# Cross-attention in turns of two rounds, its order and buffers rewritten, on one Trainium2 core

## What is computed

```python
x = layer_norm(x, g_norm);  q = x @ Wq                 # 16 heads of 64
k, v = split(context @ Wkv)                            # 128 keys per batch
k = concat([null_kv[0], k]);  v = concat([null_kv[1], v])
sim = where(mask, (q * s) @ (k * s).T, -max)           # 128 x 129 per head
out = softmax(sim) @ v;  out = out @ Wout
return layer_norm(out, g_out)
...
x = x + tanh(g_xattn[1]) * above;  x = x + tanh(g_ffn[1]) * ffn(layer_norm(x))
```

## Time and profile before

| what | value |
|---|---|
| device time, median of 3 runs | 318.1 us (316.18 to 318.48) |
| device time of the profiled execution | 316.18 us |
| its span, first to last instruction | 314.3 us |
| PE busy | 288.2 us (92%) |
| DVE busy | 242.5 us (77%) |
| ACT busy | 231.4 us (74%) |
| POOL busy | 161.3 us (51%) |

### The profile page before, as it was taken

One profiled execution on the slowest core, in us unless ns is written; L12 is line 12 of the kernel. 1 busy time (PEld: TensorE's weight loads), 2 busy tenths in 40 slices (PEclk: granted clock), 3 DMA queues, 4 the chain that ended last, 5 costly groups with the idle time before them and its releaser, 6 DMA issues.

```text
span 314.3 us, 7704 instructions
## 1 busy us (share of the span) xinstructions
PE 288.2 (92%) x2594; PEld 235.7 (75%) x2594; DVE 242.5 (77%) x726; ACT 231.4 (74%) x780; POOL 161.3 (51%) x230
## 2 busy tenths in 40 slices
PE   7688999999999869999999999999999998977765
PEld 6567768686776658889899898898998877742455
DVE  3798999999977427677787787877877878658875
ACT  2777596969899677787787877878878767429290
POOL 2124617243543115556969789686766855553200
PEclk9999999999999999999999999999999999999999
DMA  5841010002020000000000000000000000000004
GB/s 155 198 118 27 1 27 1 0 3 67 3 67 1 2 0 0 2 3 3 2 1 2 2 1 3 2 2 4 1 2 2 1 2 1 2 2 0 1 2 133
DMA packets 11478, 6.67 MB, mean 21 GB/s; under 512 B 3824, under 2 KB 10992, under 8 KB 11440
## 3 DMA queue, kind: packets, MB, share of 16 engines
q1 hardware_dynamic: 10560, 5.99, 6.9%
q10 hardware_dynamic: 880, 0.20, 0.3%
HBM read 5.14 MB, written 1.05 MB: 20 GB/s over the span
## 4 chain that ended last, share of the span: by engine, by line
PE 72%; DVE 11%; ACT 8%; issue 3%; DMA 2%; SPq 2%; POOL 1%; ACTq 0%; DVEq 0%
PE psum L1064 16%; PE psum L1191 10%; PE psum L1497 10%; PE psum L1511 9%; PE psum L1068 7%; PE psum L1070 6%; PE psum L1069 6%; DMA KT<-in_L_ffn_w_down 2%; ACT work L1055 2%; DVE hgm L2150 2%; DVE nmx L1977 2%; SPq L387 2%; PE psum L1598 1%; DVE work L1971 1%; PE psum L1288 1%
## 5 line engine op out<-in xcount | busy, mean ns | idle before, releaser
L990 ACT ACTIVATE work<-psum,nmx 128x129 f32<-128x129 f32 x256 | 83.4, 420 | 22.8 <-DVE nmx L1977 22.8
L574 POOL TENSOR_TENSOR work<-work,rden 128x512 f32<-128x512 f32 x63 | 65.7, 1042 | 46.8 <-DVE rden L1990 46.2
L1064 PE MATMUL psum<-ident,work 128*128 128x128 f32 (+2 forms) x376 | 58.8, 282 | 3.7 <-DVE work L1971 2.6
L1977 DVE TENSOR_REDUCE nmx<-psum 128x4 f32<-128x516 f32 x64 | 41.6, 689 | 25.6 <-PE psum L1191 25.4
L990 ACT ACTIVATION_READ_ACCUMULATOR work<-psum,nmx 128x1 f32 x256 | 58.9, 230 | 0.0
L1068 PE MATMUL psum<-split 97*128 97x512 f32 (+1 forms) x128 | 52.0, 406 | 1.5 <-issue 0.8
L1064 PEld LDWEIGHTS psum<-ident,work 128*128 128x128 f32 (+2 forms) x376 | 41.1, 142 | 13.5 <-issue 3.6
L1971 DVE COPY work<-psum 128x512 f32<-128x512 f32 x63 | 43.2, 686 | 4.1 <-PE psum L1064 0.3
L1070 PE MATMUL psum<-split 97*128 97x512 f32 (+1 forms) x128 | 43.3, 338 | 0.0
L1069 PE MATMUL psum<-split 97*128 97x512 f32 (+1 forms) x128 | 43.2, 338 | 0.0
L1191 PE MATMUL psum<-KT,work 64*128 64x129 f32 x512 | 37.5, 285 | 2.5 <-DVE den L1986 1.8
(11 more groups left out here) (196 smaller groups left out, 532.2 us busy)
## 6 DMA issues: line engine op xcount, KB each, us to landing
KT<-in_L_xattn_Wkv SPq DMA_DIRECT2D x2, 384.0 KB, 4.5
X<-in_x SPq DMA_DIRECT2D x1, 768.0 KB, 5.6
out_x<-X SPq DMA_DIRECT2D x3, 256.0 KB, 2.6
work<-in_ctx SPq DMA_DIRECT2D x3, 192.0 KB, 2.4
work<-in_L_xattn_Wq SPq DMA_DIRECT2D x1, 512.0 KB, 3.6
work<-in_L_xattn_Wout SPq DMA_DIRECT2D x1, 512.0 KB, 4.1
X<-in_x SPq DMA_DIRECT2D x1, 256.0 KB, 3.3
KT<-in_L_ffn_w_gate SPq DMA_DIRECT2D x1, 256.0 KB, 5.7
```

What stands on the lines that cost most here:

```text
L574: pool.tensor_tensor(sx_[:, :, 0:S], sx_[:, :, 0:S], bcast(rden[n % 2][:, :], S), ALU.mult).then_inc(p_ready.sem, 1)
L990: ins = act.activation(Sx[n % 4][:, j, :], psum[:, here, (j // 2) * K1:(j // 2 + 1) * K1], ACT.Exp, bias=nmx[n % 2][:, j:j + 1], accum_out ...
L1064: return pe.transpose(dst, src, ident[0:m, 0:m])
L1977: dve.tensor_reduce(nmx[n % 2][:, :].rearrange("p (c a) -> p c a", a=2), sim, AX_X, ALU.max, negate=True).then_inc(max_done.sem, 1)
```

## The change

The loops go over turns M of two rounds (NT = 16) in place of rounds.
- PE does in turn M: query piece of round 2M, transposes of round 2M-4, output projection of round 2M-6, transposes of round 2M-3, query piece 2M+1, output projection 2M-5, then scores of rounds 2M and 2M+1, then values of rounds 2M-4 and 2M-3. The queries are now of the round whose scores follow in the same turn.
- Transposes go to banks 4 and 5 in turn; the values of a round overwrite its bank (4 or 5) after both were copied. PTs has four buffers, oT two, Sx five.
- The null column is gone: scores have 128 columns; DVE takes the maximum of a whole round in one reduction (128 x 1024), then a small min with 0; ACT computes the null key's exponents with one ACTIVATE of 128 x 8 a round. The row sums go to SBUF (`key_sum`) in place of PSUM. A scores round waits for the exponents of its banks, in place of the denominators.
- ACT does in turn M: exponents of step 4(M-1), the two output copies of rounds 2M-6 and 2M-5, exponents of the second step, query copy, third step, query copy, fourth step, and in every second turn the copy of y.
- DVE and POOL follow the list of rounds with later places; both rounds' pair work stands on DVE behind the third denominators and ahead of the maxima.
- The last pair but one, too, is now finished on DVE after the loop, as is the last.

The diff, cut to its core (removed loops and functions stand in the printed kernel; the splitting of the key and value weights into two buffers each, whose room the new buffers reuse, is left out):

```diff
-        Sx = [work.carve(HPU * K1, n * HPU * K1).rearrange("p (h k) -> p h k", h=HPU) for n in range(4)]
-        PTs = [work.carve(HPU * S) for _ in range(2)]
-        oT = work.carve(4 * S)
+        Sx = [work.carve(HPU * S, n * HPU * S) for n in range(4)] + [late.carve(HPU * S, 0)]
+        Sx = [a.rearrange("p (h k) -> p h k", h=HPU) for a in Sx]
+        PTs = [work.carve(HPU * S) for _ in range(2)] + [late.carve(HPU * S) for _ in range(2)]
+        oT = [work.carve(4 * S), late.carve(4 * S)]
...
         hd = sb("hd", [P, G])
-        nmx = [sb(f"nmx{n}", [P, HPU]) for n in range(2)]
+
+        rmx = [sb(f"rmx{n}", [P, 2 * HPU]) for n in range(2)]
+        nmx = [sb(f"nmx{n}", [P, 2 * HPU]) for n in range(2)]
+        null_exp = [sb(f"null_exp{n}", [P, 2 * HPU]) for n in range(2)]
...
         NR = NS // 2
-        T_LAG, WO_LAG = 2, 3
-        Y_AT = 6
-        Y_STATS_AT, Y_AGGR_AT, RSTD_Y_AT, X3_AT = 6, 7, 7, 8
-        X_STATS_AT, X_AGGR_AT, RSTD_X_AT, XN4_AT, GM_AT = 9, 10, 10, 11, 12
+        NT = NR // 2
+        Y_AT, Y_STATS_AT, Y_AGGR_AT, RSTD_Y_AT, X3_AT = 9, 10, 11, 11, 12
+        X_STATS_AT, X_AGGR_AT, RSTD_X_AT, XN4_AT, GM_AT = 13, 14, 14, 15, 17
...
+            def pair_work(m):
                 if 9 <= m < 21 and m % 2 == 1:
                     down_weights((m - 9) // 2)
                 t = pair_at(m, RSTD_Y_AT)
                 if t is not None:
                     rstd_y(t)
+                    y_affine(t)
                 t = pair_at(m, X3_AT)
                 if t is not None:
                     y_gain(t)
                     residual(t)
                 t = pair_at(m, RSTD_X_AT)
                 if t is not None:
                     rstd_x(t)
-                t = pair_at(m, 1)
+                t = pair_at(m, SPLIT_AT)
+            for M in range(NT + 1):
+                for k in range(2):
+                    for n in range(4 * (M - 1) + 2 * k, 4 * (M - 1) + 2 * k + 2):
+                        if 0 <= n < NS - 1:
+                            normalise(n)
+                    pair_work(2 * M + k)
+            rstd_x(NPAIR - 3)
+            rstd_y(NPAIR - 2)
             rstd_x(NPAIR - 2)
             rstd_y(NPAIR - 1)
             rstd_x(NPAIR - 1)
...
+            def o_evac(r):
+                act.wait_ge(ot_done.sem, ot_done.at(2 * r + 2))
+                if r >= 2:
+                    act.wait_ge(wo_done.sem, wo_done.at(2 * r - 2))
+                act.activation(oT[r % 2], bank[4 + r % 2], ACT.Identity, bias=nv_col[:, 0:1]).then_inc(ot_out.sem, 1)
...
+                r, h = divmod(n, 2)
+                act.wait_ge(max_done.sem, max_done.at(r + 1))
+                if h == 0:
+                    act.activation(null_exp[r % 2][:, :], nmx[r % 2][:, :], ACT.Exp)
+                if n >= 5:
+                    act.wait_ge(pt_done.sem, pt_done.at(n - 4))
                 for j in range(HPU):
+                    at, col = 2 * h + j // 2, column(h, j)
+                    ins = act.activation(Sx[n % 5][:, j, :], bank[2 * (r % 2) + j % 2][:, at * S:(at + 1) * S], ACT.Exp,
+                                         bias=nmx[r % 2][:, col:col + 1], accum_out=key_sum[r % 2][:, col:col + 1])
                 ins.then_inc(exp_done.sem, 1)
+            for M in range(NT + 1):
+                n = 4 * (M - 1)
+                if n >= 0:
+                    exponents(n)
+                for r in (2 * M - 6, 2 * M - 5):
+                    if in_rounds(r):
+                        o_evac(r)
+                if n >= 0:
+                    exponents(n + 1)
+                if q_round(2 * M):
+                    q_round_evac(*q_round(2 * M))
+                if n >= 0:
+                    exponents(n + 2)
+                if q_round(2 * M + 1):
+                    q_round_evac(*q_round(2 * M + 1))
+                if n >= 0:
+                    exponents(n + 3)
+                t = pair_at(2 * M + 1, Y_AT)
+                if t is not None and M < NT:
                     y_evac(t)
...
+            for r in range(NR - 4, NR - 2):
+                o_evac(r)
+            act.wait_ge(pt_done.sem, pt_done.at(NS))
+            act.wait_ge(ot_done.sem, ot_done.at(NS - 4))
+            act.activation(PTs[(NS - 1) % 4], bank[2], ACT.Copy).then_inc(pt_last.sem, 1)
+            y_evac(NPAIR - 2)
+            o_evac(NR - 2)
+            o_evac(NR - 1)
...
                 if n == 0:
-                    pe.wait_ge(null_keys.sem, null_keys.at(1))
                     pe.wait_ge(q_out.sem, q_out.at(4))
-                if n >= 2:
-                    pe.wait_ge(den_done.sem, den_done.at(n - 1))
+                r, h = divmod(n, 2)
+                if r >= 2:
+                    pe.wait_ge(exp_done.sem, exp_done.at(2 * r - 2))
                 for j in range(HPU):
                     rows = slice(DH * (j % 2), DH * (j % 2) + DH)
-                    ins = pe.matmul(bank[2 * (n % 2) + j % 2][:, (j // 2) * K1:(j // 2 + 1) * K1],
+                    at = 2 * h + j // 2
+                    ins = pe.matmul(bank[2 * (r % 2) + j % 2][:, at * S:(at + 1) * S],
                                     qT[rows, 2 * hg + j // 2, (b % 2) * S:(b % 2 + 1) * S],
-                                    KTb[rows, 2 * hg + j // 2, b, :], start=True, stop=True)
+                                    KTb[rows, 2 * hg + j // 2, b, 0:S], start=True, stop=True)
                 ins.then_inc(sim_done.sem, 1)
...
             scores(0)
+            scores(1)
             def p_transposes(n):
+                r, h = divmod(n, 2)
                 if n < NS - 1:
                     pe.wait_ge(p_ready.sem, p_ready.at(n + 1))
-                    if n >= 1:
-                        pe.wait_ge(pt_out.sem, pt_out.at(n))
                 else:
                     pe.wait_ge(p_last.sem, p_last.at(1))
+                if n == NS - 4:
                     pe.wait_ge(q_out.sem, q_out.at(RPP * NPAIR))
+                elif n > NS - 4:
+                    pe.wait_ge(exp_done.sem, exp_done.at(NS - 2 if n < NS - 1 else NS))
+                elif r % 2 == 1:
+                    pe.wait_ge(pt_out.sem, pt_out.at(n - 1))
+                elif r >= 2:
+                    pe.wait_ge(ot_out.sem, ot_out.at(r - 1 + h))
                 for j in range(HPU):
-                    ins = transpose(bank[4 if n < NS - 1 else 6][:, j * S:(j + 1) * S], Sx[n % 4][:, j, 0:S])
+                    ins = transpose(p_bank(n)[:, j * S:(j + 1) * S], Sx[n % 5][:, j, :])
                 ins.then_inc(pt_done.sem, 1)
...
+                elif r % 2 == 0:
+                    pe.wait_ge(pt_out.sem, pt_out.at(2 * r + 3))
+                else:
+                    pe.wait_ge(pt_out.sem, pt_out.at(2 * r + 2))
                 for j in range(HPU):
                     rows = slice(DH * (j % 2), DH * (j % 2) + DH)
-                    at = (n % 2) * 2 * S + (j // 2) * S
-                    ins = pe.matmul(bank[5 if n < NS - 1 else 0][rows, at:at + S], V[:, b, HPU * hg + j, :],
-                                    PTs[n % 2][:, j * S:(j + 1) * S], start=True, stop=True)
+                    at = h * 2 * S + (j // 2) * S
+                    ins = pe.matmul(bank[4 + r % 2][rows, at:at + S], V[:, b, HPU * hg + j, :],
                 ins.then_inc(ot_done.sem, 1)
...
                         pe.wait_ge(ld_wo2.sem, ld_wo2.at(16))
                     else:
-                        pe.wait_ge(y_out.sem, y_out.at(t))
+                        pe.wait_ge(exp_done.sem, exp_done.at(NS))
...
+            def queries(r):
+                if q_round(r):
                     pe.wait_ge(xs_ready.sem, xs_ready.at(t + 1))
                     pe.wait_ge(q_out.sem, q_out.at(q_count(t, hg) - 1))
                     for c in range(2):
                         ins = q_proj(t, 2 * hg + c, bank[6][:, c * 2 * S:(c + 1) * 2 * S])
-                if in_rounds(m - WO_LAG):
-                    out_proj(m - WO_LAG, 0)
+            for M in range(NT + 1):
+                queries(2 * M)
+                both(round_transposes, 2 * M - 4)
+                both(out_proj, 2 * M - 6)
+                both(round_transposes, 2 * M - 3)
+                queries(2 * M + 1)
+                both(out_proj, 2 * M - 5)
+                if M == NT:
+                    p_transposes(NS - 4)
+                both(round_scores, 2 * M)
+                both(round_scores, 2 * M + 1)
+                both(round_values, 2 * M - 4)
+                both(round_values, 2 * M - 3)
+            p_transposes(NS - 3)
             p_transposes(NS - 2)
+            both(out_proj, NR - 4)
-            for h in range(2):
-                out_proj(NR - 1, h)
+            both(out_proj, NR - 3)
+            both(round_values, NR - 2)
+            both(round_values, NR - 1)
+            both(out_proj, NR - 1)
...
                 dve.tensor_scalar(ms0[:, 3:6], bank[4][:, 0:3], 1.0 / (I0 * D), SCALE_FLOOR, ALU.mult,
                                   ALU.max).then_inc(setup_v.sem, 1)
...
             def p_evac(n):
```

(64 more changed lines are left out.)

216 lines of the change are left out of this document (72 added, 144 removed).

## The result

The changed kernel takes 332.93 us (median of 4 runs, 331.68 to 336.41), the kernel before 318.29 beside it (4 runs, 316.18 to 320.8): a ratio of 1.0524, 95% interval 1.047 to 1.0579. It is slower, as forecast, but by 14.6 us in place of 5.4, and lies above the range. The profiled execution took 331.68 us; by the forecast's own sum it should have taken 321.6. So 10.1 us are to be found.

What follows compares the result with a forecast made beforehand. PE's own work and a ring through scores, maxima and transposes bound the kernel, nearly equal. After the change, 14 turns of 9.49, delays of 7.0, start and end came to plus 5.4 us: median 323.5, range 320.5 to 325.5.

Steps and rivals of the forecast that it cites:

- The sign: Whole kernel: slower, 323.5 us against a median of 318.1; slower by over 1% was given 0.62.
- Ring 1: Fifth buffer's return: ACT's twelve exponents and two query copies delay PE's second scores; a turn is T + 8.73, 9.49 us.
- sixteen reads a turn with 0.02 us either way: ACT's reads of row sums, now in SBUF: spacing kept at 0.30 us, bound 0.2 either way on a turn.
- a backlog: ACT's chain of exponents: ACT falls 0.02 us behind with each exponent, so 5.1 taken in place of 4.9.
- T: Start of a turn's first transposes on PE, from its first query product: at least 0.75 us, six query products.
- The clock: Rival at the start: PE's idle drops the clock to 1.2 GHz, or the query copy is late; 327 us, chance 15%.
- Ring 2: From DVE's maxima to the next turn's first transposes, 3.70 us; pair work in front makes turns 0.62 too long.
- T': Start of the next turn's first transposes, D + 3.70 - (T + 8.73): 1.38 us after odd turns.
- D: Start of DVE's maxima in a turn: T + 6.4 in odd turns, after pair work that waits for POOL.
- Ring 3: POOL's chain over two turns: 20.1 us from odd T to odd T, leaving 0.49 delay, 1.29 in turns 9 and 11.
- The sum of the delays: Added turn length from DVE's and POOL's late work: 6.55 us in turns 7 to 14.
- The drains: PE's changes of product kind: three a turn for six, minus 0.45 us; rival that they are all: 307, chance 3%.

Runs made afterwards that it cites:

- experiment 5: The changed kernel with a sixth buffer Sx, so exponents wait for the transposes of the step six before, not five: 328.25 us, ratio 1.0355.
- experiment 2: The changed kernel without the sums of the rows, the denominators taking a constant in their place: 322.78 us, ratio 1.0176.
- experiment 1: The kernel before with one edit, the sums of the rows going to a small SBUF tile in place of PSUM: 318.43 us, ratio 1.0007.
- Experiment 4: The changed kernel with statistics of X and the next norm one round later, so DVE never asks for POOL's work of the same turn: 328.84 us, ratio 1.0355.

## Why the prediction was wrong, point by point

- **The sign and the mechanism were right.** Ring 1 binds, at the second scores; experiment 5 takes it away, experiment 2 lets it fall below PE's work.
- **The failed step is a term of Ring 1: "sixteen reads a turn with 0.02 us either way"**, taken at nothing. Measured: 0.042 us each, beyond the bound. ACT's chain from its start to the last read's end was 4.9 by the rows and 5.1 with a backlog; the backlog did not show, eleven spacings with 0.042 make 4.9 + 0.46 = 5.36, and 5.38 was measured (156.00 to 161.38). Against the 5.1 of the sum that is 0.28 us a turn, 3.6 us in turns 2 to 14. The Trainium skill, ScalarE: Activation LUTs, section Step-by-step, names PSUM as the faster destination of an ACTIVATE; experiment 1 agrees for the read of the accumulator, the one destination that it changes, and gives the size. It deserved more than a bound guessed around zero.
- **The other terms of the turn** were each a little short: T 0.81 for 0.75, the wait for the transposes 0.69 for 0.65, the semaphore 0.14 for 0.12, and PE's part from the second scores on 2.99 for 2.87, since I had taken 1.09 - 0.11 from the scores to the values, where 1.09 was measured. That is 0.24. With ACT's 0.28 it is 0.52 a turn, 6.8 us in turns 2 to 14: two thirds of the miss.
- **The clock** was a rival at 3 us of doubled work. It fell where the rival said and cost 2.0 us in the trace (0.9 ahead of turn 2, 1.1 in it), since part of the doubled work lies beside ACT's. The rival's time, 327, still held the forecast's Ring 1, so it was short too. The other 0.5 us that are lost ahead of turn 2 fit sixteen exponents at 0.34 in place of 0.32 (0.4, an estimate).
- **Ring 2** had the right wait (1.00 us for `rstd_x`), but T' after odd turns is 1.85 and not 1.38. D in turn 9 is T + 7.31 for T + 6.4: the pair work starts 0.27 later, by the longer spacing, the wait is 0.1 shorter, and 0.7 come from the norm that took 1.06 beside POOL's normalise; 7.31 + 3.70 - 9.21 (the turn less its T, 8.73 in the forecast) gives T' = 1.80.
- **Ring 3** was too strong in its share: odd turns have T = 1.4 or 0.8 where I had 1.2 to 2.0. A longer plain turn gives POOL more room; that this is the reason was not tested apart. The sum of the delays is right (6.4 for 6.55) because Ring 2 took more and Ring 3 less: two errors against each other, thus luck. Experiment 4 shows that the waits, not POOL's load, make most of them.
- **The last turns** (turn 15 and the start of 16) were 1.3 us longer and the tail 0.35. Turn 15 took 12.12 for 10.0, with PE idle for 1.78 at its end until ACT had copied the output; from turn 16's start to the last denominators it took 6.9 for 7.7. A plain turn's 0.52 is in it once; the rest I did not test apart.
- **The drains:** half of them go, as forecast: PE's own turn is 9.15 (experiment 2; forecast 9.0) against 9.66 for two rounds before. All of this gain, 0.5 us a turn, was there and was covered by ACT.

## What to carry to other kernels

When work per engine shrinks, ask which buffer's return now sets the turn: a fifth buffer that comes free only with the turn's first transposes tied ACT's twelve exponents to PE's first work, and a sixth gave back 0.5 us a turn. Where an operand moves from PSUM to SBUF, price it on the engine that writes it and on the one that reads it, by an edit of the old kernel alone: it may be free there and decide in the new order. Pair work on an in-order engine has two deadlines, the one before it and the one behind it, and of the four positions tried here only the split one kept both.
